# Two attention layers, two gated networks: the output projection of attended tiles moved between the last group's scores

## The reference

```
x = x + attn_a(norm(x))    # 16 query heads, 4 key/value heads, rotary, biases bq bk bv bo, causal
x = x + ffn(norm(x))       # gated network, 2048 hidden, 4-bit weights with scales
x = x + attn_b(norm(x))    # 16 heads, causal, no bias
x = x + ffn(norm(x))       # the same weights again

attn:  softmax(mask(q k^T / 4)) v, heads joined -> attended;  attended @ Wo.T (+ bo)
ffn:   (gelu(x Wg^T) * (x Wu^T)) Wd^T
```

## Time and profile before

| | us |
|---|---|
| median of 3 runs (1884.41 to 1886.56) | 1885.96 |
| the profiled execution, its own time | 1884.86 |
| its span in the trace | 1882.9 |
| layer a: last value product ends, first gate matmul starts | 652.96, 691.20 |
| layer b: the same two moments | 1561.87, 1594.18 |

### The profile page before, as it was taken

The page is one execution under the profiler, slowest core; times in us unless marked ns, Lnnn a source line. Parts: engine busy times, 40 slices in busy tenths (PEclk is TensorE's granted clock), DMA queues, the critical chain, the costliest instruction groups (busy, mean ns, idle before and its releaser), DMA issues. The chain is left out here.

```text
span 1882.9 us, 34092 instructions
## 1 busy us (share of the span) xinstructions
PE 1758.3 (93%) x13822; PEld 1129.6 (60%) x13822; DVE 1158.9 (62%) x1702; ACT 956.6 (51%) x1901; POOL 545.7 (29%) x466
## 2 busy tenths in 40 slices
PE   7799999999999879999988899999999997899998
PEld 5554444555444468888876544455544445788887
DVE  6445777677786267554555567776777634754554
ACT  2132566666778624444432245777667773344443
POOL 5211366766777522333330010000000000233332
PEclk9785889999999979999998889999999998999999
DMA  5102313415111041000003224060150003300000
GB/s 131 51 26 26 44 48 66 78 44 78 43 43 40 35 197 72 1 1 0 0 1 117 72 36 68 2 87 6 26 67 2 2 2 121 148 12 1 11 11 11
DMA packets 49391, 86.04 MB, mean 46 GB/s; under 512 B 20856, under 2 KB 34936, under 8 KB 46984
## 3 DMA queue, kind: packets, MB, share of 16 engines
q1 hardware_dynamic: 44472, 67.84, 15.7%
q0 software_dynamic: 4256, 15.78, 2.7%
q10 hardware_dynamic: 528, 0.52, 0.1%
HBM read 55.02 MB, written 28.84 MB: 45 GB/s over the span
## 5 line engine op out<-in xcount | busy, mean ns | idle before, releaser
L1071 DVE TENSOR_REDUCE chunk_max<-ring 128x2 f32<-128x1024 f32 (+3 forms) x640 | 674.4, 1064 | 281.6 <-PE ring L856 166.3
L976 ACT ACTIVATE probs<-ps_s 128x512 f32<-128x512 f32 (+3 forms) x1280 | 624.0, 534 | 348.4 <-PE ps_s L887 182.8
L1406 POOL TENSOR_TENSOR inter_lo<-inter,inter_hi 128x512 fp32r<-128x512 f32 x128 | 165.4, 1292 | 910.7 <-ACT inter_hi L1351 910.7
L856 PE MATMUL ring<-unit_rounded 63*128 63x512 f32 (+3 forms) x640 | 249.7, 488 | 25.5 <-DVE chunk_max L1071 8.1
L856 PE MATMUL ring<-region_rounded 63*128 63x512 f32 (+3 forms) x640 | 255.0, 447 | 5.2 <-DVE chunk_max L1071 4.5
L882 PE MATMUL ps_s<-unit_rounded 64*128 64x512 f32 (+3 forms) x640 | 254.0, 448 | 4.9 <-ACT probs L976 4.2
L882 PE MATMUL ps_s<-region_rounded 64*128 64x512 f32 (+3 forms) x640 | 228.9, 441 | 4.3 <-ACT probs L976 4.2
L882 PEld LDWEIGHTS ps_s<-unit_rounded 64*128 64x128 f32 x640 | 113.7, 197 | 139.7 <-ACT probs L976 107.2
L899 PE MATMUL ps_o<-probs,unit_plain 128*32 128x256 f32 (+1 forms) x2304 | 188.7, 401 | 0.3 <-issue 0.3
L1380 DVE SCALAR_TENSOR_TENSOR gelu_a<-gelu_a,ps_g 128x512 f32<-128x512 f32 x128 | 88.0, 687 | 159.2 <-ACT gelu_a L1332 158.8
L1332 ACT ACTIVATE gelu_a<-ps_g 128x512 f32<-128x512 f32 x128 | 76.5, 598 | 213.1 <-PE ps_u L94 213.1
(11 more groups left out here) (184 smaller groups left out, 2955.0 us busy)
## 6 DMA issues: line engine op xcount, KB each, us to landing
w_mlp<-w_scr SPq DMA_DIRECT2D x32, 768.0 KB, 15.0
w_scr<-region_rounded POOLq DMA_DIRECT2D x16, 768.0 KB, 3.9
region_rounded<-q_scr SPq DMA_DIRECT2D x24, 256.0 KB, 8.2
q_scr<-region_rounded SPq DMA_DIRECT2D x16, 192.0 KB, 2.6
unit_rounded<-q_scr SPq DMA_DIRECT2D x12, 256.0 KB, 8.8
q_scr<-region_rounded SPq DMA_DIRECT2D x8, 384.0 KB, 3.5
k_scr<-region_rounded SPq DMA_DIRECT2D x8, 384.0 KB, 3.5
v_scr_b<-region_plain SPq DMA_DIRECT2D x4, 768.0 KB, 3.7
```

The source lines that it names most:

```text
L856: op = pe.matmul(out[:, h, 0:w], qt[g][plain[h], p, q0:q0 + P], kt[g][plain[h], p % NKP, c * TW:c * TW + w], start=True, stop=c < t)
L976: act.activation(pr[n % NPR][:, h, w0:TW], src[:, 0:TW - w0], ACT.Exp, scale=SCALE).then_inc(s_e, 1)
L1071: dve.tensor_reduce(mp[rank[y[1:3]] % 2][:, qb, 2 * p:2 * p + 2, c], ring[n % 2][:, :, 0:w], AX.X, ALU.max).then_inc(s_rd, 1)
L1406: pool.tensor_tensor(il[n % NI][:, :], ti[n % 2][:, :], ih[n % NI][:, :].bitcast(F32), ALU.subtract).then_inc(s_il, 1)
```

## The change

`output_phase` and its barrier are gone. Its work becomes entries of the plan: `AT` (turn half a tile, two blocks, of `attended`), `OP` (its 12 matmuls and the add to `x`), for each tile of the last group, behind that tile's O, whose delay goes from 3 to 1 there. For tile 3, `MS` (statistics and scales), `MN` (normalize) and `MT` (turn and split) follow, so the network's first tile is now tile 3 and is ready when its program starts. All of these go through `ring`. The high and low parts go to `xnt`, which is now allocated for the whole kernel and doubles as the operand buffer of the even groups. `WP` fetches the first two weight chunks into free columns of `xnt` at the first score of tile 2. POOL adds `bo` in four operations between weight chunks 4 to 7. The wait for the last stores moves from POOL to SP, ahead of the 14 + 2 remaining loads. In the network, tile 3 comes first, then tile 0 unrolled, then a loop of two.

```diff
@@ attention_plan
+    def projected(t):
+        out = [("AT", t, 0), ("AT", t, 1), ("OP", t, 0), ("OP", t, 1)]
+        return out + [("MS", t), ("MN", t), ("MT", t)] if t == NT - 1 else out
...
-                        turns.append([("O",) + done[:2], 3])
+                        turns.append([("O",) + done[:2], 3 if done[0] < NG - 1 else 1])
+                        if done[0] == NG - 1:
+                            turns += [[y, 2 + k] for k, y in enumerate(projected(done[1]))]
...
+                if (g, t, kb, h) == (NG - 1, NT - 2, 0, 0):
+                    plan += [("WP", n) for n in range(PRE)]
...
-    return order, plan + [o for o, _ in turns] + [("O",) + order[-1]]
+        plan += [o for o, _ in turns[:2]]
+        turns = turns[2:]
+    return order, plan + [o for o, _ in turns] + [("O",) + order[-1]] + projected(order[-1][1])
@@ attention_block, SP
+                elif y[0] == "WP":
...
+                    sp.wait_ge(per["s_st"][n], 16)
+                    sp.dma_start(xnt_[:, n, :, 2 * TW:2 * TW + WCH].bitcast(F32),
+                                 per["w_scr"][n, :, :].rearrange("p (a n) -> p a n", a=2)).then_inc(per["s_pre"][n], 16)
@@ TensorE
+                elif y[0] == "AT":
+                    t, a = y[1:]
+                    if a == 0:
+                        pe.wait_ge(s_rd, ringed[("O", NG - 1, t)] + 1)
+                    out = half_turned(slot(y))
...
+                elif y[0] == "OP":
+                    n = out_of[y]
+                    pe.wait_ge(s_rd, ringed[("AT",) + y[1:]] + 1)
+                    out = slot(y)
...
+                elif y[0] == "MT":
+                    out = tile_turned(slot(y))
+                    for b in range(BT):
+                        pe.wait_ge(ln.s_xn, NB + b + 1)
...
@@ ScalarE
+                elif y[0] == "AT":
+                    n = out_of[("OP",) + y[1:]]
+                    act.wait_ge(s_rf, ringed[y] + 1)
+                    if n >= 2:
+                        act.wait_ge(s_rf, ringed[("OP",) + att_halves[n - 2][1:]] + 1)
+                    act.activation(att_part(n, 0).rearrange("p k (b n) -> p b k n", b=BT // 2), half_turned(ring[ringed[y] % 2]),
+                                   ACT.Copy).then_inc(s_h, 1)
@@ GpSimd
+                def add_bias(j):
+                    t = j - BO_AT
+                    if 0 <= t < NT:
+                        xs = x[:, t * BT:(t + 1) * BT, :]
+                        pool.tensor_tensor(xs, xs, per["bo"][:, :].unsqueeze(1).to_broadcast([P, BT, D]), ALU.add).then_inc(s_bo, 1)
@@ VectorE
+                elif y[0] == "OP":
+                    dve.wait_ge(s_rf, n + 1)
+                    if rope:
+                        dve.wait_ge(s_bo, NT)
+                    xs = x[:, half_blocks(y), :]
+                    dve.tensor_tensor(xs, xs, ring[n % 2][:, 0, :].rearrange("p (b d) -> p b d", d=D), ALU.add).then_inc(s_rd, 1)
+                elif y[0] == "MS":
+                    dve.wait_ge(s_rd, ringed[("OP", y[1], 1)] + 1)
+                    ln.stats(dve, y[1])
+                    ln.scales(dve, y[1], y[1] + 1)
...
-def output_phase(nc, io, per, layer):
...
@@ mlp_phase
+            for b in range(2):
+                sp.wait_ge(per["s_st"][b], 16 * NF // 2)
+            for n in list(range(PRE, NF)) + list(range(PRE)):
...
-            for b in range(BT):
-                ln.turn(pe, b)
-            ln.wait_tile(pe, 0)
...
+                    if beside and n < PRE:
+                        pe.wait_ge(per["s_pre"][n], 32 if store else 16)
...
             tile(0)
-            ln.wait_tile(pe, NT - 1)
-            with pe.Fori(1, NT) as i:
+            ln.wait_all(pe)
...
+            tile(1)
+            with pe.Fori(2, NT) as i:
```

More of the change, by code:

```diff
@@ L79, in start_from_one @@
         eng.sem_inc(sem, ONE)
-def hold(eng, per, sem, value):
-    eng.wait_ge(sem, ONE + value)
-    eng.sem_inc(per["held"], 1)
 def split3(pe, out, lhs, rhs, start, stop):
@@ L132, in __init__ @@
         self.s_ld = [t.sem(f"s_dq_ld{i}") for i in range(2)]
-        self.s_st = [t.sem(f"s_dq_st{i}") for i in range(2)]
+        self.s_st = per["s_st"] = [t.sem(f"s_dq_st{i}") for i in range(2)]
         self.s_x, self.s_c, self.s_wv, self.s_hl = (t.sem(n) for n in ("s_dq_x", "s_dq_c", "s_dq_wv", "s_dq_hl"))
@@ L211, in values @@
                            self.st[b][:, :, :].bitcast(F32).rearrange("p a n -> p (a n)")).then_inc(self.s_st[b], 16)
-        for b in range(2):
-            pool.wait_ge(self.s_st[b], 16 * NF // 2)
+            between(j)
 class NormT:
@@ L311 @@
 LATE = 2
+PRE = 2
+BO_AT = 4
 def projection(t, shared):
@@ L547, in attention_block @@
         nat = Carve(praw, None).take((3, D))
-        nat_late = t_.sb("nat_late", [P, 4, D]) if rope else None
-        xnt = [early.take((2, KC, TW), F32R) for _ in range(2)]
-        xn = early.take((BT, D))
+        nat_late = t_.sb("nat_late", [P, 4, D])
+        xt = [early.take((2, KC, TW), F32R) for _ in range(2)]
+        xn = nat_late
         NST = 3 if rope else 2
@@ L1262, in _ @@
                 ov = io["out"].rearrange("o (b p) d -> p (o b) d", p=P)
-                with sp.Fori(0, NT) as i:
-                    hold(sp, per, s_dx, i + 1)
-                    sp.dma_start(ov[:, bass.ds(i * BT, BT), :], per["x"][:, bass.ds(i * BT, BT), :]).then_inc(s_out, 16)
+                for i, at in enumerate(tiles):
+                    sp.wait_ge(s_dx, ONE + i + 1)
+                    sp.dma_start(ov[:, at * BT:(at + 1) * BT, :], per["x"][:, at * BT:(at + 1) * BT, :]).then_inc(s_out, 16)
                 sp.wait_ge(s_out, 16 * NT)
@@ L1270, in _, with weight @@
             start_from_one(pe, [s_gu, s_d])
-            for b in range(BT):
-                ln.turn(pe, b)
-            ln.wait_tile(pe, 0)
+            def weight(i, n, part, at):
+                if isinstance(i, int) and i == 0 and n < PRE:
+                    return ln.xnt[:, n, part, 2 * TW + at.start:2 * TW + at.stop]
+                return w[:, n, part, at]
             def down(i, n):
@@ L1302, in tile @@
                             o = (2 * m + k) * P
-                            last = split3(pe, out[:, :], (w[:, n, 0, o:o + P], w[:, n, 1, o:o + P]),
+                            last = split3(pe, out[:, :], (weight(i, n, 0, slice(o, o + P)), weight(i, n, 1, slice(o, o + P))),
                                           ln.parts(k, cols), k == 0, k == KC - 1)
@@ L1311, in _ @@
             tile(0)
-            ln.wait_tile(pe, NT - 1)
-            with pe.Fori(1, NT) as i:
+            ln.wait_all(pe)
+            for n in range(PRE):
+                pe.wait_ge(s_w[n], 32 if store else 16)
+            tile(1)
+            with pe.Fori(2, NT) as i:
                 tile(i)
@@ L1321, in _ @@
             start_from_one(act, [s_sq, s_th, s_ih])
-            for b in range(BT):
-                ln.high(act, b)
             def tile(i):
-                beside = isinstance(i, int)
+                beside = isinstance(i, int) and i == 0
                 def first(n):
@@ L1353, in _ @@
             tile(0)
-            with act.Fori(1, NT) as i:
+            tile(1)
+            with act.Fori(2, NT) as i:
                 tile(i)
@@ L1360, in _ @@
             start_from_one(dve, [s_arg, s_gl, s_i, s_dx])
-            ln.stats(dve, 0)
-            ln.scales(dve, 0)
-            ln.norm(dve, 0)
-            for b in range(BT):
-                ln.low(dve, b)
             def add(i):
                 dve.wait_ge(s_d, ONE + i * NF + NF)
-                x = per["x"][:, bass.ds(i * BT, BT), :]
+                first = tiles[i] * BT if isinstance(i, int) else (i - 1) * BT
+                x = per["x"][:, bass.ds(first, BT), :]
                 dve.tensor_tensor(x, x, ps_d[:, :, :], ALU.add).then_inc(s_dx, 1)
             def tile(i):
-                beside = isinstance(i, int)
+                beside = isinstance(i, int) and i == 0
                 for n in range(NF):
@@ L1413, in attend @@
         attention_block(nc, io, per, layer)
-        output_phase(nc, io, per, layer)
 def build(nc, io):
@@ L1433, in build @@
             "w_scr": nc.dram_tensor("w_scr", (NF, P, 2 * WCH), F32, kind="Internal").ap(),
-            "held": t.sem("s_held"), "s_w": [t.sem(f"s_w{n}") for n in range(NF)],
+            "s_pre": [t.sem(f"s_w_first{n}") for n in range(PRE)], "s_w": [t.sem(f"s_w{n}") for n in range(NF)],
         }
```

158 lines of the change are left out of this document (76 added, 82 removed).

## The result

The changed kernel takes 1856.8 us (median of four runs, 1852.8 to 1860.2) against 1886.3 us for the kernel before: a ratio of 0.9851, 95% interval 0.9824 to 0.9879, or 29.4 us. A second series gave 1857.8 against 1886.2 us, 0.9854 (0.9833 to 0.9874). The forecast was 1860, with 1850 to 1872 as range. The profiled execution of after has a span of 1858.3 us and is the longest of its four; against the 1882.9 us of before it is only 24.6 us shorter. Executions of one kernel on one chip differ by up to 22 us and go with the mean granted clock (the kernel before: 1868.6 us at 0.961, 1890.2 at 0.942); sizes are therefore taken from marks within one trace, with the medians beside them.

A forecast was written before the change was run, and what follows sets the result against it. TensorE was taken to set the pace in the scores, with passages of 38.2 and 32.3 us where little is busy. Gains of 14.4, 8.5 and 2.6 us make 25.5, from 1885.96 to 1860 us; range 1850 to 1872.

The forecast's parts named there:

- rival A: Whole kernel: moved work delays the scores but the passages before the networks shrink; 25.5 us gained, 1860 us; chance 0.52.
- push by tile 3's work: Tile 2's scores, per layer: 5.3 us of moved TensorE work plus 2 us (0 to 5) of stalls.
- push by tile 2's work: Tile 1's scores, per layer: 4.1 us of moved work, taken as 3.3 us (2 to 5).
- tail: Last value product to first gate matmul in the changed kernel, per layer: 10.1 us (9 to 11.5).
- passage: Last value product to first gate matmul: 38.2 and 32.3 us before; push plus tail, 23.8 us, after.
- first chunk, clock: Network's first weight chunk: 5.3 us at half clock, 2.65 at full; half the saving counted, 1.3 us per layer.
- Edits at nothing: POOL's bias, WP loads, remaining weights, tile 1's unrolled code and the store wait moved to SP: costed at zero.
- B: Ring entries within the scores: stalls of 0.4 us at each of 24 per layer; 1870 us; chance 0.13.
- C: Where ring entries and M pairs alternate: TensorE stops 1.5 us per entry, 1896 us; chance 0.05.
- D: Ahead of layer a's network: POOL's gap stays, 5 us, 1865 us; chance 0.09.
- E: Between scores: half of 12 us of moved matmuls per layer hide in TensorE's waits, 1848 us; chance 0.11.
- F: Plan: entries pile up and fall behind the last score, some 3 us of latencies per layer; 1866 us; chance 0.06.

The follow-up runs named there:

- the tripled matmuls: Changed kernel with each projection matmul of tile 3 issued three times over; 1875.3 us.
- the run without them: Changed kernel with statistics, normalization and turning of the first tile (MS, MN, MT) put behind everything else; 1876.7 us.
- the last run: Changed kernel with 16 idle matmuls at each of the network's two waits and tile 0's sums turned ahead of tile 1's second projected half; 1850.6 us.
- the first run with idle matmuls in the network: Changed kernel with 16 idle matmuls at each of the network's two waits; its edit to the tail left the order as it was; 1851.0 us.
- the two runs on the clock: Changed kernel with most of tile 0's projection left out, 1857.9 us; kernel before with 24 idle matmuls in each network's head, 1887.0 us.
- the idle matmuls in the head: Kernel before with 24 idle matmuls of 512 columns in the head of each network; 1887.0 us.
- the last two kernels: Changed kernel with idle matmuls at the network's two waits, tail order unchanged, 1851.0 us, and with tile 0's sums turned earlier, 1850.6 us.
- the run without steps: Changed kernel with a tile's moved entries placed one right behind the other instead of one entry per step; 1889.5 us.

## Why the prediction was right

The forecast was 1860, the result 1856.8, by the account that was forecast (rival A).

| step | forecast, us per layer | measured, layers a and b |
|---|---|---|
| push by tile 3's work | 7.3 | 6.55 and 6.53 |
| push by tile 2's work | 3.3 | 4.47 and 4.46 |
| push by tile 1's work | 3.1 | 3.34 and 3.36 |
| push in all | 13.7 | 14.36 and 14.35 |
| tail | 10.1 | 9.65 and 9.64 |
| passage | 23.8 | 24.00 and 23.99 |
| gain of the passage | 14.4 and 8.5 | 14.2 and 8.3 |
| first chunk, clock | 1.3 | 2.13 and 2.44 |

**The push.** That moved matmuls aren't free was the step on which the size of the passage's gain rests, and the tripled matmuls show it to 0.1 us. The parts are off in both directions. For the stall by MS and its neighbours I took 2 us between 0 and 5; 0.9 is what the run without them leaves. For tile 2 I counted 4.1 us of matmuls as 3.3, since TensorE had 0.6 us free and ACT was near full; it cost 4.46, all of it and 0.4 of waiting. The errors cancel.

**The tail.** The sum hit by two errors as well. The 24 matmuls ran at full clock in both layers (3.1 us from 1565.52 to the end of the last, where I took 4.0); the rest of the chain took 6.55 us where I had 6.05. DVE's addition for tile 1, which I had nowhere, stands ahead of the normalization of tile 0 (1561.99 in the rows above), and the second half of tile 1 ahead of the turn: putting the turn first won 0.4 us in the last run.

**The clock.** The step that was mis-sized: I took half of a possible saving because I couldn't tell whether 24 matmuls bring the clock back. In both traces of the changed kernel they don't have to: the clock doesn't fall in the tail, and the sign that I had named, projection matmuls of tile 0 partly 0.22 us apart, is missing. Where it did fall there (layer a with tripled matmuls, layer b of the first run with idle matmuls in the network), it was back before the tail's end, and the first chunk took 2.81 and 2.82 us. Measured 2.1 and 2.4 us per first chunk, 4.6 in place of 2.6, and 5.0 over the first tile; the two runs on the clock show that those matmuls carry it. That is 2.4 of the 3.9 us between the forecast gain of 25.5 and the medians' 29.4; the rest is within what separates the two series (29.4 and 28.4).

**Edits at nothing.** POOL's bias in four parts, the moved waits and tile 1's unrolled code left no mark: the copies of the sums lie 1.45 to 1.60 us behind before's throughout layer a, up to the last group, and the network's second tile takes 67.4 us in layer a where it took 67.3. The third chunk's gate comes 1.0 us late (685.25 in layer a), but by the row it waits for DVE's product of the first chunk, as it did before (0.94 us), not for weights. The prefetch I priced only as an edit that costs nothing; it is worth 6.3 us per layer.

**The rivals.** *B*: no stall of the size that it needs; it appears (10 us in layer b, more in layer a) when the steps are taken out. *C*: the same stalls, in some executions with the clock behind them, bring the median to 1889.5 us, where the gain is gone; I had looked for them in the ring's places, and the price per entry was not their measure. *D*: the gap is gone because the last store lies 16.3 us ahead; its size was right, its cause half right (a wait and a closing). *E*: out by the tripled matmuls. *F*: priced at 3 us per layer; the run with all entries behind the last score costs 9.7. What I had left out are statistics ahead of subtractions on DVE, and the clock.

## What to carry to other kernels

Moving work between steps of an engine that is full doesn't make the work cheaper; it hides the waits of its chain, and the gain is the length of the passage that empties minus the full price of what is moved in. Count that price one to one, give each hand-over between engines a step of its own, and put a long chain on DVE where TensorE has something else to do. After that look at the clock at the start of the next stage: here 20 matmuls taken out of the tail made it 2 us shorter and the first tile behind it 1.7 and 3.0 us longer.

## What the runs showed of the hardware that I had not expected

**A stall that came with added matmuls.** Four of the twelve experiments stop TensorE for 3.0 to 3.9 us in layer b, between 1349 and 1383 us, waiting for nothing that the profile shows. They are the four with matmuls added to TensorE's program: the tripled projection, the idle matmuls in the head, and the two with idle matmuls in the network's waits. In the first run with idle matmuls in the network, timeline:

```profile
1353.71 0.79 PE L908 MATMUL ps_s<-xnt 64*128 64x512 f32 x1 [3.87 <-issue]
```

The stretch of that stall (the last two columns are DMA share and GB/s):

```profile
1349.00:1353.80 4.80, 0.93 (x13) 0.34 (x12) 0.83 (x1) 0.39 (x1) 0.00 (x0) 0.64 0.97 105
```

The DMA engines are 0.97 busy at that moment with loads for the next group. The instruction queue q8 of these four moves one packet more than that of the kernel they are made from (98 against 97, 104 against 103); in the other eight the count is unchanged and no such stall appears. The length of the program alone is not the cause: the changed kernel moves six packets more than the kernel before (103 against 97) and has no such stall. The DMA queues of the first run with idle matmuls in the network, from 1349.80 to the restart (packets, MB, share of the engines):

```profile
q1 hardware_dynamic: 400, 0.39, 95.7%
q8 instruction: 1, 0.02, 3.1%
```

All four traces have one packet of q8 in the last 3.8 to 4.0 us ahead of the restart and none in the 24 us before that, while q1 moves data. The changed kernel has none for 22 us at this place either (1344.1 to 1365.8), without a stall. That TensorE waits for instructions whose fetch stands behind the data is my reading; it fits these rows, but none says what the packet holds. The stall gives back 3.1 of the some 6 us that the idle matmuls in the head had won over the two first tiles (85.85 to 82.05 and 84.58 to 82.16 us), and 4 us in the last two kernels.

**A small DVE instruction held up by POOL.** Timeline of the run without steps, layer a, while POOL works on weight chunks:

```profile
606.41 2.78 POOL L182 TENSOR_SCALAR region_plain<-region_plain 128x768 f32<-128x768 int32 x1
...
608.51 0.16 DVE L521 TENSOR_TENSOR ln_small<-ln_small 128x4 f32<-128x4 f32 x1
...
610.18 1.80 POOL L186 TENSOR_TENSOR region_plain<-region_plain 128x768 f32<-128x768 f32 x1
610.34 1.66 DVE L521 TENSOR_TENSOR ln_small<-ln_small 128x4 f32<-128x4 f32 x1
```

The same instruction takes 0.16 us or 1.66, and then it ends with POOL's. The four normalizations took 4.18 us in place of 1.38. This is why that stall is 10.8 us in layer a and 5.6 in layer b, where POOL is idle. The Trainium skill, "SBUF — State Buffer", Who interferes with whom, states a lock on the ports that the two engines share, held for a whole instruction; the rows at 610.18 and 610.34 agree. The row at 608.51 ran unhindered while the POOL instruction of 606.41 was still under way (to 609.19), so here not every such pair collided (a profile's spans on POOL are rough).
